# A gated cross-attention and mixture kernel: the corner of the decay matrix cleared by a minimum ahead of the products, and the first batch's loads moved one stage up

## The reference, cut to what matters

```python
log_f_cum = cumsum(log_sigmoid(fg))                   # forget gates, over time
log_D = tril(log_f_cum[s] - log_f_cum[t]) + ig[t]     # -inf above the diagonal
D  = exp(log_D - max(log_D))                          # decay matrix
C  = (q @ k.T) / sqrt(32) * D
h  = (C / (max(abs(C.sum(-1)), exp(-max_log_D)) + 1e-6)) @ v
hn = (h - mean(h)) * rsqrt(var(h) + 1e-6) * ln_scale
x  = x + tanh(g_xattn) * hn
```

## Time and profile before

| | |
|---|---|
| median of 3 runs | 800.06 us |
| profiled execution | 801.35 us |
| its span, first to last instruction | 799.6 us |
| TensorE (PE) busy | 682.2 us, 85% |
| VectorE (DVE) busy | 536.7 us, 67% |
| ScalarE (ACT) busy | 411.7 us, 51% |
| GpSimd (POOL) busy | 391.0 us, 49% |
| last instruction of attention (residual of round 31) | starts 313.00 us |

### The profile page before, as it was taken

The page is one execution under the profiler, slowest core; times in us unless marked ns, Lnnn a source line. Parts: engine busy times, 40 slices in busy tenths (PEclk is TensorE's granted clock), DMA queues, the critical chain, the costliest instruction groups (busy, mean ns, idle before and its releaser), DMA issues.

```text
span 799.6 us, 20108 instructions
## 1 busy us (share of the span) xinstructions
PE 682.2 (85%) x7280; PEld 595.1 (74%) x7280; DVE 536.7 (67%) x1056; ACT 411.7 (51%) x848; POOL 391.0 (49%) x595
## 2 busy tenths in 40 slices
PE   0876068888888882799999999999999999999994
PEld 0553057767677772688889998999998999999993
DVE  4762849899899997776427788533557666676750
ACT  0667246676766763554444232222556666656652
POOL 2111347888888884322112525123237575757554
PEclk9989559999999997799999999999999999999998
DMA  8883274644545512477752313233568797888854
GB/s 252 268 273 102 90 204 148 187 135 148 180 121 171 157 47 68 159 274 265 252 207 74 103 58 85 74 93 107 175 224 224 229 237 244 232 253 222 258 130 53
DMA packets 90720, 135.57 MB, mean 170 GB/s; under 512 B 16720, under 2 KB 44112, under 8 KB 90672
## 3 DMA queue, kind: packets, MB, share of 16 engines
q1 hardware_dynamic: 74128, 107.41, 40.8%
q0 software_dynamic: 7168, 17.04, 10.8%
q10 hardware_dynamic: 9376, 10.49, 4.2%
HBM read 92.32 MB, written 34.21 MB: 158 GB/s over the span
## 4 chain that ended last, share of the span: by engine, by line
PE 49%; DVE 4%; DMA 2%; POOL 2%; issue 1%; ACT 1%; POOLq 0%; ACTq 0%; DVEq 0%
PE psH L1215 30%; PE psY L1233 14%; PE psR L1260 2%; PE psT L1195 2%; DMA out<-ystage,sidx 1%; POOL out L1722 1%; PE psT L1268 1%; DMA xrows<-xn,eidx 1%; DVE w13l L1466 1%; DVE xnorm L1633 1%; PE psG L1275 1%; DVE xl L1454 1%; DVE stats L1524 1%; DVE over13h L1633 1%; ACT over13l L1402 0%
## 5 line engine op out<-in xcount | busy, mean ns | idle before, releaser
L1215 PE MATMUL psH<-xh,w13h 128*128 128x256 f32 (+1 forms) x768 | 222.8, 290 | 3.0 <-DVE w13l L1466 3.0
L1215 PE MATMUL psH<-xh,w13l 128*128 128x256 f32 (+1 forms) x768 | 216.6, 282 | 0.0
L1215 PE MATMUL psH<-xl,w13h 128*128 128x256 f32 (+1 forms) x768 | 216.0, 281 | 0.0
L1690 POOL TENSOR_TENSOR hl<-sg,hh 128x256 fp32r<-128x256 f32 (+1 forms) x96 | 79.5, 840 | 207.2 <-ACT hh L1334 206.5
L1215 PEld LDWEIGHTS psH<-xh,w13h 128*128 128x128 f32 (+1 forms) x768 | 138.5, 180 | 12.5 <-issue 7.7
L1215 PEld LDWEIGHTS psH<-xl,w13h 128*128 128x128 f32 (+1 forms) x768 | 138.9, 181 | 0.7
L1215 PEld LDWEIGHTS psH<-xh,w13l 128*128 128x128 f32 (+1 forms) x768 | 138.8, 181 | 0.0
L1460 DVE TENSOR_TENSOR sg<-sg,psH 128x256 f32<-128x256 f32 (+1 forms) x96 | 40.0, 417 | 98.3 <-ACT sg L1329 98.0
L1329 ACT ACTIVATE sg<-psH 128x256 f32<-128x256 f32 (+1 forms) x96 | 36.3, 378 | 130.8 <-PE psH L1215 126.1
L730 ACT ACTIVATE dec<-ring 128x512 f32<-128x512 f32 x128 | 73.8, 591 | 25.2 <-PE ring L634 24.8
L806 DVE SCALAR_TENSOR_TENSOR dec<-psQ,dec 128x512 f32<-128x512 f32 x128 | 79.3, 680 | 7.4 <-PE psQ L646 6.4
(11 more groups left out here) (226 smaller groups left out, 1381.8 us busy)
## 6 DMA issues: line engine op xcount, KB each, us to landing
raw<-w13T SPq DMA_DIRECT2D x64, 352.0 KB, 4.1
gcT<-ctxT ACTq DMA_DIRECT2D x8, 1024.0 KB, 6.5
kT<-ctxT SPq DMA_DIRECT2D x16, 512.0 KB, 5.2
ctxs<-ctx SPq DMA_DIRECT2D x16, 512.0 KB, 3.4
xn<-xnorm SPq DMA_DIRECT2D x16, 512.0 KB, 4.4
out<-xres SPq DMA_DIRECT2D x16, 512.0 KB
raw<-w2T SPq DMA_DIRECT2D x16, 512.0 KB
qst<-qT_all SPq DMA_DIRECT2D x14, 512.0 KB, 6.1
```

Of the source, the lines that this page charges most:

```text
L1215: last = nc.tensor.matmul(psH[m][0:n, v, :], w[wp][:, c, col:col + n], x[xp][:, c, :], start=(c == 0 and k == 0), stop=(c == DC - 1 and k ...
L1690: nc.gpsimd.tensor_tensor(hs[u.p][1][0:n, m, :], sg[0:n, m, :], hs[u.p][0][0:n, m, :].bitcast(F32), ALU.subtract).then_inc(hl_ready, 1)
```

## The change

The corner is now cleared ahead of the products, by a minimum with a tile that holds 3.0e38 where the value is to stay and 0 where it is to vanish. It is done twice a round, for head groups k and k + 1 at a time, with k = 0 and 2; each is linked (VectorE waits for its end). The semaphore `cleared` and the tiles `zeros` and `none` are gone. The tiles of the first batch's keys and values are made one level further out, and their loads are issued in the gate stage, behind the loads of the gates; in the attention stage `load_em(0)` moves ahead of `load_decay(0, 1)`.

```diff
-            c.link(nc.gpsimd.memset(g.none[:, :], 0.0))
-            c.link(nc.gpsimd.memset(g.zeros[:, :], 0.0))
-            c.link(nc.gpsimd.memset(g.corner[:, :], 0.0))
+            c.link(nc.gpsimd.memset(g.corner[:, :], 3.0e38))
             c.link(nc.gpsimd.affine_select(out=g.corner[:, :], in_=g.corner[:, :], compare_op=ALU.is_ge,
-                                           fill=1.0, base=SPARE, pattern=[[1, P - SPARE]], channel_multiplier=-1))
+                                           fill=0.0, base=SPARE, pattern=[[1, P - SPARE]], channel_multiplier=-1))
...
                 sp.dma_start(head[:, k, :, :], d.gt.rearrange("w b h t -> (b h) w t")[k * P:(k + 1) * P]).then_inc(head_in[k], 16)
+            sp.dma_start(g.kT0[:, :, :], d.ctxT[0].rearrange("(c p) t -> p c t", p=P)).then_inc(g.kT_in[0], 16)
+            sp.dma_start(g.ctx0[:, :, :], d.ctx[0].rearrange("(c p) d -> p c d", p=P)).then_inc(g.ctx_in[0], 16)
...
             def load_keys(b, u):
-                sp.dma_start(kT[u][:, :, :], ...).then_inc(kT_in[u], 16)
+                if b > 0:
+                    sp.dma_start(kT[u][:, :, :], ...).then_inc(kT_in[u], 16)
...
             load_decay(0, 0)
             load_keys(0, 0)
-            load_ctx(0, 0)
+            load_em(0)
             load_decay(0, 1)
-            load_em(0)
             load_ctx(1, 1)
...
                 pe.wait_ge(v_ready, 2 * b + c + 1)
-                pe.wait_ge(cleared, 4 * i + r + 1)
...
-            def clear(i, r):
+            def clear(i, r, k, use):
                 c, lo = r % 2, P - 32
-                dve.wait_ge(c_done, 16 * i + 4 * r + 4)
-                nc.vector.tensor_tensor(g.none[:, 0:1], g.none[:, 1:2], g.none[:, 2:3], ALU.mult)
-                wide = lambda t: t[lo:P, :].rearrange("p (o t) -> p o t", o=1).broadcast_to([32, NH, P - SPARE])
-                nc.vector.copy_predicated(dec[c][lo:P, :, :, SPARE:P].rearrange("p k g t -> p (k g) t"),
-                                          wide(g.corner).bitcast(U32), wide(g.zeros)).then_inc(cleared, 1)
+                dve.wait_ge(emptied, use + 1)
+                ends = dec[c][lo:P, k:k + 2, :, SPARE:P].rearrange("p k g t -> p (k g) t")
+                wide = g.corner[lo:P, :].rearrange("p (o t) -> p o t", o=1).broadcast_to([32, NH // 2, P - SPARE])
+                c_.link(nc.vector.tensor_tensor(ends, ends, wide, ALU.min))
...
                 for k in range(4):
+                    if k % 2 == 0:
+                        clear(i, r, k, decay_use(i, r, k + 1))
                     weigh(i, r, k, decay_use(i, r, k))
-                clear(i, r)
```

More of the change, by code:

```diff
@@ L503, in attention_stage @@
         a = Pools(nc, ctx)
-        kT = [a.sb(f"kT{u}", [P, DC, S]) for u in range(2)]
+        kT = [g.kT0, a.sb("kT1", [P, DC, S])]
         qst = g.qst
-        ctxs = [a.sb(f"ctxs{u}", [P, 2, D]) for u in range(2)]
+        ctxs = [g.ctx0, a.sb("ctxs1", [P, 2, D])]
         emb = a.sb("emb", [P, DC, P])
@@ L523, in attention_stage @@
         (filled, emptied, v_ready, qk_done, c_done, inter_done, back_done, sq_ready, o_taken, red_done, ve_ready,
-         x_done, t_ready, kk_ready, qsc_ready, state_zero, weights_set, y_ready, state_done, state_taken, cleared, chain, pch, ach) = map(
+         x_done, t_ready, kk_ready, qsc_ready, state_zero, weights_set, y_ready, state_done, state_taken, chain, pch, ach) = map(
             a.sem, ["at_" + n for n in (
@@ L527, in attention_stage @@
                 "red_done", "ve_ready", "x_done", "t_ready", "kk_ready", "qsc_ready", "state_zero", "weights_set", "y_ready", "state_done",
-                "state_taken", "cleared", "chain",
+                "state_taken", "chain",
                 "pool", "act")])
-        ctx_in = [a.sem(f"at_ctx_in{u}") for u in range(2)]
+        ctx_in, kT_in = g.ctx_in, g.kT_in
         em_in = a.sem("at_em_in")
-        kT_in = [a.sem(f"at_kT_in{u}") for u in range(2)]
         q_in = [a.sem(f"at_q_in{u}") for u in range(2)]
@@ L575, in load_keys @@
             def load_keys(b, u):
-                sp.dma_start(kT[u][:, :, :], d.ctxT[bass.ds(b, 1)].rearrange("b (c p) t -> p (b c) t", p=P)).then_inc(kT_in[u], 16)
+                if b > 0:
+                    sp.dma_start(kT[u][:, :, :], d.ctxT[bass.ds(b, 1)].rearrange("b (c p) t -> p (b c) t", p=P)).then_inc(kT_in[u], 16)
                 if b < 2:
@@ L805, in weigh @@
                 dk = dec[c][:, k, :, :].rearrange("p a t -> p (a t)")
-                weighed = nc.vector.scalar_tensor_tensor(out=dk, in0=psQ[:, k, :], scalar=SCALE, in1=dk, op0=ALU.mult, op1=ALU.mult)
-                weighed.then_inc(c_done, 1)
-            def clear(i, r):
+                nc.vector.scalar_tensor_tensor(out=dk, in0=psQ[:, k, :], scalar=SCALE, in1=dk,
+                                               op0=ALU.mult, op1=ALU.mult).then_inc(c_done, 1)
+            def clear(i, r, k, use):
                 c, lo = r % 2, P - 32
-                dve.wait_ge(c_done, 16 * i + 4 * r + 4)
-                nc.vector.tensor_tensor(g.none[:, 0:1], g.none[:, 1:2], g.none[:, 2:3], ALU.mult)
-                wide = lambda t: t[lo:P, :].rearrange("p (o t) -> p o t", o=1).broadcast_to([32, NH, P - SPARE])
-                nc.vector.copy_predicated(dec[c][lo:P, :, :, SPARE:P].rearrange("p k g t -> p (k g) t"),
-                                          wide(g.corner).bitcast(U32), wide(g.zeros)).then_inc(cleared, 1)
+                dve.wait_ge(emptied, use + 1)
+                ends = dec[c][lo:P, k:k + 2, :, SPARE:P].rearrange("p k g t -> p (k g) t")
+                wide = g.corner[lo:P, :].rearrange("p (o t) -> p o t", o=1).broadcast_to([32, NH // 2, P - SPARE])
+                c_.link(nc.vector.tensor_tensor(ends, ends, wide, ALU.min))
             def take(i, r):
@@ L862, in drain @@
                 residual(i, r)
-            run(dve, c_, 4, step, drain)
+            run(dve, c_, 12, step, drain)
         @block.gpsimd
@@ L1815, in build @@
             g.coef = c.sb("coef", [P, D])
+            g.kT0, g.ctx0 = c.sb("kT0", [P, DC, S]), c.sb("ctxs0", [P, 2, D])
+            g.kT_in = [c.sem(f"at_kT_in{u}") for u in range(2)]
+            g.ctx_in = [c.sem(f"at_ctx_in{u}") for u in range(2)]
             g.qst = [c.sb(f"qst{u}", [P, DC, S]) for u in range(2)]
@@ L1822, in build @@
             g.corner = c.sb("corner", [P, P - SPARE])
-            g.zeros = c.sb("zeros", [P, P - SPARE])
-            g.none = c.sb("none", [P, 4])
             with ExitStack() as gates:
```

## The result

The changed kernel takes 814.93 us (median of 4, 813.89 to 815.66) against 799.77 us before: ratio 1.0188, 95% interval 1.0171 to 1.0206. It is slower by 15.2 us; forecast were 814.5 us and slower. Its profiled execution took 813.89 us (span 811.8).

A forecast was written before the change was run, and what follows sets the result against it. The prediction took a ring of waits across engines in attention, not VectorE's total, as the bound. Minima +14.8 us less 0.4 for the moved loads gave +14.4 on 800.06, so 814.5 us, range 804 to 822.

The forecast's parts named there:

- The ring: Attention: a cycle of tight waits through GpSimd, VectorE, TensorE and ScalarE, 12.21 or 12.31 us per two rounds, sets the time.
- Rival D: Attention: VectorE's total work decides, so the change is faster, 785.5 us; chance 0.06.
- E: Attention: the minima hide behind an unseen wait and only the moved loads count, 799.0 to 799.6 us; chance 0.05.
- Removing the old clearing: Behind the products each round: dropping L813 and L815, 0.43 + 0.58 us, was taken at nothing.
- The minima are on the ring: Between residual and last product: both minima lengthen odd rounds, +14.8 us in sum; even rounds add nothing.
- What a minimum takes: VectorE, each minimum: 0.21 us of work, 0.34 us with edges and lost overlap (bounds 0.26 to 0.43).
- What stands behind it: VectorE, between each minimum and the next product: a link of 0.03 us.
- first kind of ring: Rings with a pause of some 0.4 us ahead of GpSimd's key scaling: minimum 2 waits for that scaling, +0.80 us.
- The port: VectorE instructions with two SBUF inputs wait for GpSimd's running instruction, then precede its next; the second ring gets +1.22 us.
- C: First ring: GpSimd's lift takes the port before the waiting minimum, 6.8 us more, 821 us; chance 0.07.
- B: Attention: the minima never meet a long GpSimd instruction, +8.9 us, 809 us; chance 0.18.
- The loads: Start of attention: moved loads start the first queries 1.05 us earlier, net gain 0.43 us (bounds 1.05 gained, 0.6 lost).

The follow-up runs named there:

- noclear: The changed kernel with the minima left out and nothing clearing the corner (output not the reference's): 795.83 us, ratio 0.9948.
- minonly: The kernel before with only the two minima in place of the old clearing, first batch's loads not moved: 823.09 us, ratio 1.0301.
- early: The kernel before with only the first batch's key and value loads moved to the gate stage, old clearing kept: 798.22 us, ratio 0.9984.
- waits: The changed kernel with the products' waits moved ahead of the minimum in front of them: 815.61 us, ratio 1.0188.
- hoist0: The changed kernel with minimum 0 of the next round moved ahead of the residual add, into VectorE's idle time: 809.58 us, ratio 1.0119.
- late_min: The changed kernel with the residual add one round later on VectorE: 807.44 us, ratio 1.0084.
- late_old: The kernel before with the moved loads and old clearing, and the residual add one round later on VectorE: 808.36 us, ratio 1.0091.
- nf_old: The kernel before with the moved loads and old clearing, GpSimd normalising ahead of lift and query scaling in even rounds: 812.32 us, ratio 1.0162.
- nf_none: The changed kernel without any clearing, GpSimd normalising ahead of lift and query scaling in even rounds: 797.56 us, ratio 0.9976.
- nf_min: The changed kernel with GpSimd normalising ahead of lift and query scaling in even rounds: 824.31 us, ratio 1.0306.
- minonly2: A repeat of minonly, the same kernel measured once more: 818.59 us, ratio 1.0225.

## Why the prediction was right

By its steps:

- **What bounds.** The ring, not VectorE's total. Shown: 4.4 of 26 us of VectorE's work were taken out (noclear) and the rings stayed. Rival D fell with it, and E with minonly.
- **Removing the old clearing is worth nothing.** Shown to 0.7 us of attention (noclear against early).
- **The minima are on the ring, in odd rounds only.** Shown: +1.00 and +1.35 us a ring of two rounds (one of the fourteen +1.55), all of it between the residual and the queries of an odd round.
- **What a minimum takes.** 0.205 us at the median (forecast 0.21). It starts 0.02 to 0.04 us behind the instruction in front of it and does not overlap it, on the last 32 partitions, as the Trainium skill's rule of the held instruction has it (VectorE: DVE Perf Modes, Two Vector instructions with no wait between them); no run had the minimum on the same partitions as its neighbours, so that the partitions are the reason is not shown. Nor does the old pair bear it out quite as the prediction says: L815 stands on the last 32 partitions, but L813 stands on all 128 (its shape is 128x1), and what starts apart there is L815 from L813 and L813 from the products, the latter with a wait between.
- **What stands behind it** was mis-sized: 0.03 us forecast, 0.21 and 0.12 measured in the hardware loop. That made the first kind of ring 0.20 longer than forecast and the second 0.13. It cancelled in part against the next term. In the first kind of ring the pause pushed minimum 2 up to the end of the key scaling (205.36 + 2.47 against 2.52), so its wait for the port (forecast 0.26) vanished. The sum was +0.80 + 1.22 = 2.02 for four rounds, and +2.35 came, 2.3 us more over seven times four rounds; the other 0.5 is the first ring with its 13.73. In waits, with the pause gone, it was 13.01 + 13.55 - 12.21 - 12.31 = 2.04.
- **The port.** Forecast: the second ring's minimum waits for the lift, and the first ring's gets in before it. Both as forecast; C fell, and B too. The waits of the first kind of ring can be seen in waits and hoist0, where minimum 2 waits for the key scaling and the lift that follows the scaling keeps its 1.01 us (208.14 in hoist0). hoist0 is the test of the port.
- **The loads.** Forecast 0.43 us, bounds 1.05 and -0.6; measured 1.5 us at the first lift of round 2 in the changed kernel and 2.5 in early, outside the bounds. The step was right up to the queries of round 1 (0.41 earlier). What was left out is the clock: TensorE was at the upper one by the queries of round 1, and they took 1.17 us and not 2.09, 0.92 of the gain.
- **The memsets and the other stages** were put at nothing. The profiles differ there by 4.0 us, of which a part may be the change's, as said with the result.
- **The signs.** All but one came: the last residual stands at 326.48 us (327 forecast, though the stage began 2.7 us earlier), the rings are 13.21 and 13.66 (13.0 and 13.5), minimum 2 lasts 0.2 to 0.9, VectorE is busy 20.18 us of the stretch of rows 1 and not 23.84. But its idle time ahead of the residual did not grow (10.1 us in 20 waits, before 9.6 in 21); what grew is that ahead of the take, for the squares (19.0 in 14, before 2.4 in 8).
- **The sum** is right in part by luck. Attention got 16.2 us longer where 14.4 were forecast (rings 2.8 us too little, the start 1.1 too little gain), and the medians moved by only 15.2, by what lies outside of attention.

## What to carry to other kernels

The engine with the highest busy share need not be the one on the ring: follow one recurring wait back to itself, and price an added instruction by whether it lies on that path, a removed one likewise. A short VectorE instruction with two SBUF inputs costs its own 0.2 us only where no long GpSimd instruction runs; elsewhere it costs the rest of that instruction too (0.66 and 0.83 us beside the lift). An idle stretch of VectorE ahead of what it waits for is the place for it (hoist0 got back 5.4 of the 15 us; late_min got back 7.5 by moving the residual, and no order with the minima reached the kernel before), and a new order has to be costed with its port waits before it is believed.

## What the hardware showed that was not expected

- A wait for VectorE's own last instruction, followed by instructions that wait on counts kept in registers, cost 0.21 us (two such waits behind it) and 0.12 (one) in the hardware loop, and 0.04 with none behind it (waits) or in rounds written out. That working out the counts takes this time is my reading, and waits bears it out. In round 31 of the changed kernel minimum 0 starts at 313.52 for 0.20 us, and the product at 313.76.
- The port works both ways and even on small instructions. L839's residual in the kernel before (201.95, 0.69 long) stretches GpSimd's product of 0.22 us behind it, which ends 0.07 after the residual; in hoist0 the same product takes up to 0.75:

```profile
202.06 0.65 POOL L921 TENSOR_TENSOR sm<-sm 128x16 f32<-128x16 f32 x1
```

- TensorE's clock at the start of attention. In the kernel before the granted clock is 0.50 up to 113 us; in the changed kernel it rises at about 107, 6 us into the stage. How long the 32 products of round 1's queries take then goes with TensorE's idle time just ahead of them. They take 1.17 us behind 0.54 to 0.62 us of it (early, noclear, late_old, nf_old, nf_none), 1.03 (hoist0), 1.08 (nf_min) and 1.16 (the changed kernel), and 1.96 behind 1.32 (late_min), 2.04 behind 1.54 (waits), 2.09 behind 1.73 (minonly2), 1.36 behind 1.84 (minonly). In waits the granted clock is 0.91 from 109 to 111 us and 0.50 from 111 to 113, so it had risen and fell again. In the kernel before the idle time is 0.32 and they take 2.09, for there it had not risen. The queries of the kernel before and of waits:

```profile
112.31 2.09 PE L646 MATMUL psQ<-qst,kT 32*128 32x128 f32 x32 [0.32 <-DVE dec L806]
```

```profile
110.53 2.04 PE L645 MATMUL psQ<-qst,kT 32*128 32x128 f32 x32 [1.54 <-DVE dec L801]
```
